# Order of the scalar engine in a decoder layer: the next row's exponentials behind this row's quantised copies

## The reference

```python
x = _layernorm(x + attention(x, ...))                      # x1 in the kernel
x = _layernorm(x + wkv(time_decay, time_first, k=x, v=ctx_2048))   # x2

def wkv(...):            # per channel, along the 256 tokens
    # y_t = (e1*aa + e2*v) / (e1*bb + e2), with running sums aa and bb
    # aa' = decay*aa + exp(k)*v ;  bb' = decay*bb + exp(k)

def bitlinear(x, w):     # feed-forward, twice, with a gelu between
    xn = layer_norm(x)
    x_hat = clip(xn * 128 / max|xn|) * max|xn| / 128
    return x_hat @ ternary(w).T
x = _layernorm(x + bitlinear(gelu(bitlinear(x, w_fc)), w_proj))
```

## Time and profile before

| what | value |
|---|---|
| median of 3 runs | 1492.68 us (1492.28 to 1495.35) |
| the profiled execution | 1491.6 us |
| its span, first to last instruction | 1489.6 us |
| mean granted TensorE clock | 0.956 |
| busy: TensorE, VectorE, ScalarE, GpSimd | 92%, 69%, 44%, 18% |

### The profile page before, as it was taken

One profiled execution on the slowest core, in us unless ns is written; L12 is line 12 of the kernel. 1 busy time (PEld: TensorE's weight loads), 2 busy tenths in 40 slices (PEclk: granted clock), 3 DMA queues, 4 the chain that ended last, 5 costly groups with the idle time before them and its releaser, 6 DMA issues.

```text
span 1489.6 us, 21291 instructions
## 1 busy us (share of the span) xinstructions
PE 1374.5 (92%) x6882; PEld 1073.8 (72%) x6882; DVE 1022.9 (69%) x1845; ACT 649.2 (44%) x1198; POOL 267.2 (18%) x192
## 2 busy tenths in 40 slices
PE   8999999999999999999999999999838798877986
PEld 6888888878888888888888888888624444443543
DVE  5666665665666666666657665655689888898874
ACT  5443434342443434343333433343326765666645
POOL 2111100110010100011011000100224434344320
PEclk9999999999999999999999999999958898888889
DMA  5011211120110111011010100010000011100000
GB/s 191 8 57 36 70 35 56 35 73 19 50 42 21 42 35 42 21 42 46 24 42 21 42 7 28 7 35 29 15 29 15 15 42 42 42 13 30 28 15 29
DMA packets 14430, 54.93 MB, mean 37 GB/s; under 512 B 2112, under 2 KB 2112, under 8 KB 12096
## 3 DMA queue, kind: packets, MB, share of 16 engines
q1 hardware_dynamic: 14400, 54.55, 10.6%
HBM read 50.35 MB, written 4.19 MB: 37 GB/s over the span
## 4 chain that ended last, share of the span: by engine, by line
PE 76%; DVE 12%; issue 6%; ACT 4%; DMA 0%; SPq 0%; DVEq 0%; POOL 0%; ACTq 0%; POOLq 0%
PE bank L327 16%; PE bank L329 16%; PE bank L328 15%; PE bank L376 4%; PE bank L378 4%; PE bank L377 4%; PE bank L483 2%; PE bank L342 2%; PE bank L358 2%; PE bank L366 2%; DVE hid L1154 2%; DVE bb L1009 2%; DVE amax_h L1144 1%; DVE aa L1024 1%; DVE den L1030 1%
## 5 line engine op out<-in xcount | busy, mean ns | idle before, releaser
L327 PE MATMUL bank<-x_hi,w_hi 128*128 128x512 f32 x1024 | 413.5, 404 | 7.3 <-DVE x_lo L838 6.5
L329 PE MATMUL bank<-x_hi,w_lo 128*128 128x512 f32 x1024 | 401.8, 392 | 0.0
L328 PE MATMUL bank<-x_lo,w_hi 128*128 128x512 f32 x1024 | 399.9, 391 | 0.0
L823 DVE TENSOR_TENSOR resid<-resid,bank 128x512 f32<-128x512 f32 x256 | 173.6, 687 | 150.6 <-PE bank L378 149.9
L1256 POOL TENSOR_TENSOR sq_sum<-sq_sum,o_sq 128x512 f32<-128x512 f32 x64 | 104.6, 1634 | 872.6 <-ACT o_sq L591 872.6
L327 PEld LDWEIGHTS bank<-x_hi,w_hi 128*128 128x128 f32 x1024 | 193.5, 189 | 46.2 <-issue 8.9
L329 PEld LDWEIGHTS bank<-x_hi,w_lo 128*128 128x128 f32 x1024 | 192.8, 188 | 43.1
L328 PEld LDWEIGHTS bank<-x_lo,w_hi 128*128 128x128 f32 x1024 | 193.6, 189 | 37.2
L829 DVE SCALAR_TENSOR_TENSOR gated<-g_t,bank 128x512 f32<-128x512 f32 x64 | 44.0, 687 | 176.2 <-PE bank L358 176.2
L586 ACT ACTIVATE v_t<-bank 128x512 f32<-128x512 f32 x64 | 38.3, 598 | 185.9 <-PE bank L329 185.9
L470 PE MATMUL bank<-tern,xq_hi 128*128 128x512 f16 x256 | 103.4, 404 | 15.5 <-DVE xq_lo L1041 15.5
(11 more groups left out here) (153 smaller groups left out, 2515.6 us busy)
## 6 DMA issues: line engine op xcount, KB each, us to landing
w_raw<-w_ffn SPq DMA_DIRECT2D x32, 512.0 KB, 3.3
raw<-w_heads SPq DMA_DIRECT2D x15, 1024.0 KB, 4.8
raw<-w_heads SPq DMA_DIRECT2D x17, 256.0 KB, 2.8
x_in<-x_rows SPq DMA_DIRECT2D x8, 512.0 KB, 3.3
val<-ctx_t SPq DMA_DIRECT2D x8, 512.0 KB, 3.5
out<-y_out SPq DMA_DIRECT2D x8, 512.0 KB, 2.8
resid<-x_t SPq DMA_DIRECT2D x3, 1024.0 KB, 9.4
resid<-x_t SPq DMA_DIRECT2D x4, 256.0 KB, 4.0
```

The source lines that it names most:

```text
L327: mm(PJ[j % 2][:, :], a, c, start=kt == 0, stop=False)
L328: mm(PJ[j % 2][:, :], a, d, start=False, stop=False)
L329: last = mm(PJ[j % 2][:, :], b, c, start=False, stop=kt == KT - 1)
L823: tt(resid[:, 4 * g + t, :], resid[:, 4 * g + t, :], YB[t % 2][:, :], ALU.add).then_inc(y_added, 1)
```

## The change

In ScalarE's `row`, the call `exps(b + 1)` moves behind the two calls of `split_xq(b, t)`. Nothing is added or removed on any engine, and no other engine's order is changed.

```diff
                 first_norms(b, final)
                 if not final:
                     copy_key(b + 1)
+                for t in range(BT):
+                    split_xq(b, t)
+                if not final:
                     exps(b + 1)
-                for t in range(BT):
-                    split_xq(b, t)
                 act.wait_ge(scfc_ok, b + 1)
```

More of the change, by code:

```diff
@@ L724, in row @@
                     copy_key(b + 1)
-                    exps(b + 1)
                 for t in range(BT):
                     split_xq(b, t)
+                if not final:
+                    exps(b + 1)
                 act.wait_ge(scfc_ok, b + 1)
```

## The result

| | before | after |
|---|---|---|
| median | 1492.48 us (4 runs, 1490.22 to 1495.35) | 1504.97 us (4 runs, 1503.88 to 1505.16) |
| the profiled execution | 1491.6 us | 1505.13 us |
| its span, first to last instruction | 1489.6 us | 1503.3 us |

The ratio is 1.0081, with a 95% interval of 1.0063 to 1.0099: the change makes the kernel slower by 12.5 us, between 9.4 and 14.8. The forecast was 1508.4, in a range of 1502 to 1515.

The account below looks back on a forecast made before the run. The prediction took VectorE's chain to bound the rows: six loop rows at +2.41 us (14.5) and row 0 at +1.2 gave +15.7 us, added to 1492.68 for 1508.4 us, range 1502 to 1515.

Parts of the forecast that it names:

- `xq_hi` earlier: ScalarE's copies in loop rows end at 1255.79 instead of 1258.41; VectorE's path to the `bb` scans is 4.1 us earlier.
- The exponentials later: On ScalarE in loop rows, table load and four `ek1` follow the copies and end 2.95 us later, delaying the scans.
- E: The end of ScalarE's four `ek1` exponentials, forecast to move from 1255.86 to 1258.81 in loop rows.
- The collision: VectorE's four `bb` scans and GpSimd's products start together; scans take 6.64 us instead of 2.42, ending 2.41 us later per loop row.
- two faster ones: Scans and products do not hinder each other, or TensorE decides the time: each -13.9 us, 1478.8; chance together 0.06.
- the 4.23 us from which it decides: Length of VectorE's four `bb` scans below which the kernel would be faster than before, in the no-hindrance rival.
- order that differs: At the `bb` scans: GpSimd first at E, 1510.9 us, chance 0.10; or two scans ahead of a product, 1505, chance 0.08.
- nothing for TensorE's clock: TensorE's wait ahead of L483 grows from 6.67 to some 12 us; its clock is already at half, so nothing added.
- a spread of 0.8 us a row: Allowance for TensorE's clock returning at other points of each row: 5 to 6 us in all.
- The shares of the page: The page's TensorE share of 92% was assigned to the attention stage and set aside, the change lying in rows behind it.

## Why the prediction was right

The mechanism held term by term, and one term of the sum was mis-sized.

- **`xq_hi` earlier.** Expected 8.34 us into the row for the end of the copies, measured 8.42; `xq_lo` with 1.83 us of idle time (some 1.8 expected), `sc_fc` at 0.22 (0.2).
- **The exponentials later.** E moved by 3.03 us (2.95). VectorE's new wait is 2.08 us (about 2).
- **The collision.** The scans take 6.67 us (6.64) and the products 2.71 and 2.78 (2.8 each). The end of the scans moved by 2.43 us (2.41) in the row shown, and by 1.05 in row 0 (1.2). The experiments show the cause, which the prediction had from one row of before: with E where the change puts it, products shorter by 2.16 us take 2.18 us off the scans, and one product less takes 2.13.
- **The rivals.** None of the two faster ones: the scans are far above the 4.23 us from which it decides, and TensorE's wait at L470 is gone without a gain, while its wait ahead of L483 grew from 6.67 to 12.93 us. VectorE was first at E in the loop too, by 0.13 us in the row shown, and the second scan waits for `t1` in every row, so neither order that differs came about.
- **The term that was mis-sized: nothing for TensorE's clock.** The forecast was +15.7 us, the profiled executions lie 13.5 apart. The rows of before and after, by their first instruction, are longer by 1.31, 2.41, 2.41, 1.82, 2.01, 1.63 and 1.91 us (rows 0 to 6), 13.50 in all, and by nothing in row 7. From the end of the scans to the next row it is 31.22 us in after and 31.83 in before, in the row shown. Most of the difference is VectorE's idle time ahead of the second tile's `hq_lo`: in the seven rows 0, 0, 0.26, 0.50, 0.62, 0.68 and 0.72 us before, 2.8 together, and 0.16, 0, 0.27, 0, 0.24, 0 and 0.22 after, 0.9 together. It is largest where TensorE is still at the lower clock through `turn_back` and into the second `turn_hq`. `turn_back` took 1.87 to 1.91 us in rows 2 to 6 of before. In rows 1, 3 and 5 of after the clock had come back ahead of it, and it took 1.04, as here in row 3.

```profile
1293.29 1.04 PE L447 MATMUL bank<-ident,num 128*128 128x128 f32 x8
```

I had taken this as a spread of 0.8 us a row and no shift; it was a shift of 1.9 us in all, in the direction of the faster end. Loop rows of after are 49.35 to 49.71 us long instead of the 49.9 forecast. With TensorE kept busy in both kernels the rows shown are 2.40 us apart, as the sum said. The last 1.0 us between 13.5 and the medians' 12.5 lies inside the spread of the runs.
- **The shares of the page.** The rows begin at about 1107 us, so they fill some 10 of the 40 slices, not the last 13. Nothing in the sum hangs on it.

## What to carry to other kernels

An engine's idle time ahead of an operand is worth only what the next operand allows: here VectorE was done with `sc_fc` 4.0 us earlier in the row, 2.6 of it won at `xq_lo`, and the scans behind it needed what had been moved back. Before a release that two engines wait for is moved, look at what they do with it: work that was spaced in time may then start together, and the price is in the one place of the trace where it already does. Where an instruction takes longer in one place than elsewhere at the same shape, look for the GpSimd instruction that ends with it; moving that one to a place where VectorE doesn't meet it was worth 10 to 12 us each on the kernel before.

## What the runs showed of the hardware

- Four scans with both inputs in SBUF took 6.64 to 6.67 us beside GpSimd's two products, in nine starts (one of before, eight of after), and 2.42 alone. In each start the second and the fourth scan took some 2.77 us and the others 0.66 to 0.69, which fits turns by whole instructions: a scan, a product, a scan, the copy, a scan, a product, a scan. The Trainium skill, SBUF — State Buffer, section Who interferes with whom, says that such a pair excludes each other for a whole instruction. The runs agree: forcing GpSimd to be first moved the end of the scans by only 0.82 us, and halving the products took 2.16 us off them and 2.18 off the scans. From the end of `ek1` to the end of the scans neither engine waits for a semaphore of the other, so engines here do not meet only through semaphores, as the first section has it.
- The hold reaches very small instructions: `sc_fc` is 128x2, and took 1.65 us beside a product and 0.22 alone. It doesn't reach every VectorE instruction: `xq_lo`, which reads one of its inputs from PSUM, took 1.29 us for two in the earlier trace rows, while GpSimd did `t1` and `t2`, and the same 1.29 in after, with GpSimd idle.
- After the same 12.93 us of idle time and ahead of the same work, TensorE's `turn_back` took 1.04 us in rows 1, 3 and 5 of after and 1.83 to 1.89 in rows 2, 4 and 6. What decides it in a given row is open.
